# Cross-attention's sums sent whole through DRAM, their reciprocals broadcast back, and the last projection one turn later

## The reference

```python
x = _layernorm(x + attn(x))                  # 16 heads of 16, causal, projections in and out
x = _layernorm(x + xattn(x, ctx_2048))       # see below
x = _layernorm(x + ffn(x))                   # 256 -> 1024 -> 256, ternary weights, 8-bit activations
# xattn: here the 64 POSITIONS are the channels and the 256 columns the tokens
q = rotary(split_heads(Wq @ x + bq)); k = rotary(split_heads(Wk @ c + bk)); v = split_heads(Wv @ c + bv)
p = softmax(q @ k.T / sqrt(8))               # 8 heads of 8 channels, 256 x 256
out = Wo @ merge_heads(p @ v) + bo
```

## Time and profile before

| | us |
|---|---|
| median of 3 runs (lowest, highest) | 562.46 (562.35, 567.57) |
| the profiled execution | 563.8 |
| its span, first to last instruction | 561.9 |
| mean granted TensorE clock in it | 0.848 of full speed |

### The profile page before, as it was taken

How to read it: one execution, slowest core, us unless ns; L and a number is a source line. 1 busy time by engine, 2 the same in 40 slices (tenths; PEclk the granted TensorE clock), 3 DMA queues, 4 the chain that set the end, 5 groups by cost and what they waited for, 6 DMA issues and landing times. The chain is left out here.

```text
span 561.9 us, 12026 instructions
## 1 busy us (share of the span) xinstructions
PE 450.6 (80%) x4162; PEld 243.0 (43%) x4162; DVE 442.4 (79%) x965; ACT 382.0 (68%) x698; POOL 289.6 (52%) x387
## 2 busy tenths in 40 slices
PE   6568799999999999999999999889877701555563
PEld 5354545555545555555555555433333200333342
DVE  2656687888988979889889798865848959999973
ACT  2222266767767667676676686687767787999972
POOL 5742565447555574475555744620032727667652
PEclk9677799999999999999999999975987875555555
DMA  6134318233242242332422323210000000000010
GB/s 217 48 97 149 97 46 248 66 92 91 57 111 67 64 110 60 90 91 60 108 69 64 106 61 82 71 56 1 3 1 1 1 0 1 10 28 19 30 37 29
DMA packets 51674, 37.07 MB, mean 66 GB/s; under 512 B 21408, under 2 KB 47648, under 8 KB 51488
## 3 DMA queue, kind: packets, MB, share of 16 engines
q1 hardware_dynamic: 51328, 36.10, 22.8%
q10 hardware_dynamic: 288, 0.23, 0.2%
HBM read 24.52 MB, written 10.49 MB: 62 GB/s over the span
## 5 line engine op out<-in xcount | busy, mean ns | idle before, releaser
L970 DVE TENSOR_REDUCE MX<-mx_b 128x2 f32<-128x512 f32 x256 | 167.8, 679 | 37.6 <-PE mx_b L581 36.4
L775 ACT ACTIVATE PB<-e_b 128x512 f32<-128x512 f32 x256 | 149.6, 592 | 64.7 <-PE e_b L609 63.8
L581 PE MATMUL mx_b<-KA,QA 48*128 48x256 bf16 x512 | 100.8, 282 | 10.3 <-DVE MX L970 10.1
L609 PE MATMUL e_b<-QA,KA 50*128 50x256 bf16 x512 | 100.9, 281 | 2.7 <-ACT PB L775 2.1
L626 PE MATMUL u_b<-PB,VA 128*32 128x256 f32 x1024 | 86.2, 404 | 3.4 <-ACT PB L775 2.9
L897 POOL TENSOR_TENSOR SP<-SP,srec 128x1024 f32<-128x1024 f32 x15 | 28.5, 1901 | 79.0 <-DVE srec L942 79.0
L581 PEld LDWEIGHTS mx_b<-KA,QA 48*128 48x128 bf16 x512 | 30.1, 95 | 88.5 <-issue 48.9
L1238 POOL TENSOR_TENSOR H<-H,row_tab 128x1024 f32<-128x1024 f32 x16 | 37.8, 2359 | 22.9 <-ACT H L1196 19.5
L1285 PE MATMUL r_b<-identh,Q 128*128 128x128 f16 x128 | 16.6, 311 | 39.5 <-ACT Q L1206 39.5
L1291 PE MATMUL z_b<-w2q,Q2T 128*128 128x256 bf16 x128 | 30.2, 417 | 19.3 <-ACT Q2T L1217 19.3
L314 POOL TENSOR_TENSOR rs<-mv,epsc 128x1 f32<-128x1 f32 x32 | 6.1, 189 | 72.5 <-DVE mv L301 50.2
(11 more groups left out here) (169 smaller groups left out, 1048.4 us busy)
## 6 DMA issues: line engine op xcount, KB each, us to landing
KA<-parts_k SPq DMA_DIRECT2D x64, 96.0 KB
QA<-parts_q SPq DMA_DIRECT2D x64, 96.0 KB
parts_q<-part_q SPq DMA_DIRECT2D x32, 128.0 KB, 2.0
parts_k<-part_k SPq DMA_DIRECT2D x16, 192.0 KB, 2.1
C<-in_ctx SPq DMA_DIRECT2D x16, 128.0 KB, 3.0
X<-in_x SPq DMA_DIRECT2D x16, 128.0 KB, 2.9
out_y<-O SPq DMA_DIRECT2D x16, 128.0 KB, 1.7
XT<-in_xT SPq DMA_DIRECT2D x15, 128.0 KB, 2.2
```

Of the source, the lines that this page charges most:

```text
L581: m = nc.tensor.matmul(mx_b[n % 2][:, D * k:D * k + D], QA[low:low + K_MAX, 2 * i.ring + b, h, P * u:P * u + P], KA[low:low + K_MAX, 2 * i ...
L609: m = nc.tensor.matmul(e_b[n % 2][:, D * k:D * k + D], KA[low:low + K_EXP, 2 * i.ring + b, h, P * sc:P * sc + P], QA[low:low + K_EXP, 2 * ...
L775: nc.scalar.activation(PB[:, n % 4].rearrange("p e t -> p (e t)"), e_b[n % 2][:, :], ACT.Exp, scale=XC ** -0.5).then_inc(e_sb.sem, 1)
L970: nc.vector.tensor_reduce(MX[:, b, e, 2 * q:2 * q + 2, u], mx_b[n % 2][:, :].rearrange("p (e s) -> p e s", e=2), AXL.X, ALU.max).then_inc( ...
```

## The change

1. `u_transpose`, `u_norm`, `att_transpose` and `at_copy` are gone. US goes whole to a DRAM tensor `u_hbm` of (32, 4, 2, 512), one DMA of 256 KB per sequence. When both have landed, one row of each group of 32 is loaded as S32 (the sums, 128x32) and eight as UV (the values, 128x256). VectorE takes reciprocals of S32 at step 6 of the next turn; they go out to DRAM (16 KB) and come back broadcast over 8 channels as RB (128x256). GpSimd multiplies UV by RB (`means`).
2. The columns of the output projection's weights are reordered on the host, and the value bias goes through the projection once, in turn 0, into the bias `xbo` (`value_bias`).
3. The projection and the second norm come one turn later, for `late` = i-2: projection at step 5, statistics at step 6, `norm2` and `square_sum` at step 9, `norm2_max` at step 10. In turn 15 they come a second time, for pair 14: steps 12, 13, 15, 15. On GpSimd `rstd` of late stands ahead of `self_norm`, and `means` of prev behind it.
4. On SyncE the new DMAs and their waits stand between the old ones; the expansion of k opens the next turn, that of q comes ahead of `max_rows(nxt, 0)`.
5. In the feed-forward block the last pair's load, reciprocals (VectorE, turn 2), projection (turn 6), statistics (turn 7) and norm (turn 8) come later; the factors at turn 13 instead of 9.
6. `identb` is built by two copies of 64 rows instead of one addition.

```diff
@@ functions of both phases @@
-        def u_transpose(pe, i, b, ps):
...
-        def att_transpose(pe, i, ps):
...
-        def at_copy(act, i, g):
...
-        def u_norm(dve, i, b, g):
...
+        u_hbm = nc.dram_tensor("u_hbm", (32, 4, 2, 2 * D), F32, kind="Internal").ap()
+        rec_hbm = nc.dram_tensor("rec_hbm", (16, D), F32, kind="Internal").ap()
+        def store_sums(sp, i, b):
+            if has(i, 1):
+                sp.wait_ge(ld_uv, 16 * i.v)
+                sp.wait_ge(ld_us, 16 * i.v)
+            wait(sp, u_sb, i, b + 1)
+            sp.dma_start(u_hbm[:, :, b].rearrange("c j x -> j c x"), US[:].rearrange("p s t -> p (s t)")).then_inc(moved[b], 16)
+
+        def load_sums(sp, i):
+            if has(i, 1):
+                wait(sp, at_sb, i.plus(-1), 1)
+            for b in range(2):
+                sp.wait_ge(moved[b], 16 * (i.v + 1))
+            flat = u_hbm.rearrange("c j b x -> c (j b x)")
+            sp.dma_start(S32[:], flat[XC:XC + 1].rearrange("c (r t) -> (c r) t", t=32)).then_inc(ld_us, 16)
+            sp.dma_start(UV[:], flat[0:XC].rearrange("c (r t) -> (c r) t", t=D)).then_inc(ld_uv, 16)
+
+        def recip_out(sp, i):
+            wait(sp, u_rec, i, 1)
+            if has(i, 1):
+                sp.wait_ge(rec_in, 16 * i.v)
+            sp.dma_start(rec_hbm.rearrange("h (k t) -> (h k) t", t=32), S32[:]).then_inc(rec_out, 16)
+
+        def recip_in(sp, i):
+            sp.wait_ge(rec_out, 16 * (i.v + 1))
+            sp.dma_start(RB[:], rec_hbm.unsqueeze(0).broadcast_to([XC, 16, D])).then_inc(rec_in, 16)
+
+        def reciprocals(dve, i):
+            dve.wait_ge(ld_us, 16 * (i.v + 1))
+            nc.vector.reciprocal(S32[:], S32[:]).then_inc(u_rec.sem, 1)
+
+        def means(pool, i):
+            pool.wait_ge(ld_uv, 16 * (i.v + 1))
+            pool.wait_ge(rec_in, 16 * (i.v + 1))
+            if has(i, 1):
+                wait(pool, xo_ps, i.plus(-1), 1)
+            nc.gpsimd.tensor_tensor(AT[:], UV[:], RB[:], ALU.mult).then_inc(at_sb.sem, 1)
@@ SyncE, body(i) @@
+                if real(prev):
+                    store_sums(sp, prev, 1)
+                if i.v >= 0 and real(j):
+                    expand_rows("k", j)
                 if i.v >= 1 and real(a):
                     load_c(a)
+                if real(prev):
+                    load_sums(sp, prev)
                 if real(i):
                     max_rows(i, 1)
                 if real(a):
                     cross_values(a)
+                if real(prev):
+                    recip_out(sp, prev)
                 if real(j):
                     store_parts("q", j)
+                if real(prev):
+                    recip_in(sp, prev)
+                if real(i):
+                    store_sums(sp, i, 0)
+                if real(j):
+                    expand_rows("q", j)
                 if real(nxt):
                     max_rows(nxt, 0)
-                if real(j):
-                    expand_rows("q", j)
...
-                if real(a):
-                    expand_rows("k", a)
@@ TensorE, body(i) @@
+                    if s == 5 and real(late):
+                        x_out_proj(pe, late, use(g_b[2], ln2, late, 1))
+                    if s == 12 and i.v == NPAIR - 1:
+                        x_out_proj(pe, prev, use(g_b[2], ln2, prev, 1))
@@ ScalarE, u_copy @@
-                    wait(act, ut_ps, i, 1)
+                    act.wait_ge(moved[0], 16 * (i.v + 1))
@@ ScalarE, body(i) @@
+                    if s == 9 and real(late):
+                        norm2(act, late)
+                        square_sum(act, late)
@@ VectorE, body(i) @@
+                    if s == 6 and real(prev):
+                        reciprocals(dve, prev)
+                    if s == 6 and real(late):
+                        norm2_stats(dve, late, 2)
+                    if s == 10 and real(late):
+                        norm2_max(dve, late)
@@ GpSimd, body(i) @@
+                if real(late):
+                    rstd(pool, ln2, late, mv2, rs2)
                 if real(a):
                     self_norm(pool, nc.gpsimd, a)
+                if real(prev):
+                    means(pool, prev)
                 if i.v == NPAIR - 1:
                     mean_power(pool, 0)
-                if real(prev):
                     rstd(pool, ln2, prev, mv2, rs2)
```

More of the change, by code:

```diff
@@ L629, in pv_quad, with value_bias @@
                 last.then_inc(pv.sem, 1)
+            def value_bias(g):
+                ps = use(g_b[g], Event(s_bias, 0), Pair(0, 0), 1)
+                pe.wait_ge(ld_cross, NCROSS)
+                nc.tensor.matmul(ps[:, 0:1], xw["o"], xb["v"], start=True, stop=True).then_inc(s_bias_ps, 1)
             def weight_total(g):
@@ L869, in body @@
                         v_copy(i.plus(4), g_b[0])
-                    if s == 15 and real(prev):
+                    if s == 15 and i.v == NPAIR - 1:
+                        norm2(act, prev)
                         square_sum(act, prev)
@@ L995, in _ @@
             dve.wait_ge(ld_att, 16)
-            nc.vector.tensor_tensor(identb[:].rearrange("p (b t) -> p b t", b=2),
-                                    ident[:, 0:HALF].unsqueeze(1).broadcast_to([P, 2, HALF]),
-                                    ident[:, HALF:P].unsqueeze(1).broadcast_to([P, 2, HALF]), ALU.add).then_inc(s_tab, 1)
+            for r in range(2):
+                own = slice(HALF * r, HALF * r + HALF)
+                nc.vector.tensor_copy(identb[own, :].rearrange("p (b t) -> p b t", b=2),
+                                      ident[own, own].unsqueeze(1).broadcast_to([HALF, 2, HALF])).then_inc(s_tab, 1)
             nc.vector.tensor_copy(maskb[:], mask.unsqueeze(1).broadcast_to([P, 8, SEQ])).then_inc(s_tab, 1)
             def body(i):
-                prev, nxt, j, a = i.plus(-1), i.plus(1), i.plus(2), i.plus(3)
+                late, prev, nxt, j, a = i.plus(-2), i.plus(-1), i.plus(1), i.plus(2), i.plus(3)
                 for s in range(16):
@@ L1221, in _ @@
                 first_values(t)
-                if t == 1:
-                    at_copy(act, last, 0)
-                if t == 5:
+                if t == 8:
                     norm2(act, last)
@@ L1251, in _ @@
             mean_power(pool, 1)
+            means(pool, last)
             rstd(pool, ln2, last, mv2, rs2)
-            mean_power(pool, 2)
             for n in range(NPAIR):
+                if n == 5:
+                    mean_power(pool, 2)
                 wait(pool, qb, Pair(0, n), 1)
@@ L1406, in _ @@
         def _(sp):
+            load_sums(sp, last)
+            recip_out(sp, last)
+            recip_in(sp, last)
             for n in range(NPAIR):
@@ L1450 @@
         own = np.arange(64 * b, 64 * b + 64)
+        summed = np.arange(XC * 4 * 2 * 2).reshape(XC, 4, 2, 2)[:, :, b].reshape(-1)
         for k, n in enumerate(XW):
-            cross_w[64 * b:64 * b + 64, k, split[b] if n in ROTATED else own] = weights[n].T
+            cols = split[b] if n in ROTATED else own
+            cross_w[np.ix_(summed if n == "o" else own, [k], cols)] = weights[n].T[:, None, :]
         for k, n in enumerate(XBIAS):
-            cross_b[split[b] if n in ROTATED else own, k] = biases[n]
+            cross_b[split[b] if n in ROTATED else summed if n == "v" else own, k] = biases[n]
     arrays = {
```

111 lines of the change are left out of this document (40 added, 71 removed).

## The result

The changed kernel takes 622.17 us (median of 4 runs, 618.0 to 625.56) against 564.62 (4 runs, 562.35 to 567.57) for the kernel before on the same chip: a ratio of 1.101, 95% interval 1.090 to 1.112. Slower was right; the size was not. I had forecast 577 us with a range up to 590, so the loss is 57.5 us where 14.6 were reckoned.

The account below looks back on a forecast made before the run. It took TensorE and VectorE as both full in a turn's first half, TensorE alone in the second. Terms -0.5 + 3.5 + 7.0 + 0 - 2.5 + 5.9 + 1.2 = +14.6 us gave 577 us, range 558 to 590.

Parts of the forecast that it names:

- The store: SyncE's 256 KB store of US: confined to 4 engines, 73 GB/s, landing 4.7 us after issue (bounds 2.0 and 7).
- It fits, with half a microsecond: Middle turns: sums and row maxima arrive in time despite the store, the sums with a margin of 0.5 us.
- behind the keys' expansion on the same engines: Load of the sums in a middle turn: there by 10.0 us into the turn, queued after the keys' expansion.
- Late sums: Rival, chance 0.13: data come a microsecond later, VectorE stands at step 6 every turn, +1 x 11, 588 us.
- The per-turn term: Each of eleven middle turns: 1.82 us longer in one half, 1.18 shorter in the other, +0.64 net, +7.0 in all.
- ScalarE hides its part: Rival, chance 0.20: step 12 is not held up by ScalarE, a turn grows 0.1 rather than 0.64 us, 571 us.
- first half: Steps 5 to 12 of a turn, TensorE and VectorE both full: self-attention's transposes start later, +1.82 us.
- The ends: Outside the middle turns: turn 0 -0.5, turn 1 +3.5, turn 13 0, turn 14 -2.5, turn 15 +5.9, feed-forward +1.2 us.
- TensorE was the only bound: Rival, chance 0.17: step 6's statistics fit into waits, a turn gains 1.3 of 1.55 us, 548 us by the median.

Follow-up runs that it names:

- e4: Changed kernel in which SyncE no longer waits for the stores and the loads of sums and values read constant tables instead: 616.02 us, ratio 1.093.
- b1: Kernel before plus only the stores of US to DRAM, in the pattern led by 4, read by nothing: 599.73 us, ratio 1.068.
- b2: As b1, the kernel before plus stores nobody reads, but with the DRAM pattern led by 128: 565.43 us, ratio 1.000.
- e1: Changed kernel with each store of US cut into four DMAs of 32 partitions: 582.63 us, ratio 1.033.
- e3: Changed kernel with the four stores of e1 and the late norm put back to its old steps: 567.82 us, ratio 1.006.
- e8: e3 with stores of 9 of each 32 partitions and the identity built by one addition: 561.83 us, ratio 0.997 against the kernel before.
- e9: e8 with the load of the values issued behind the row maxima instead of ahead: 559.34 us, ratio 0.995 against the kernel before.

## Why the prediction failed, step by step

- *The store.* Right: a quarter of the engines (share 0.25), and that a microsecond more would be felt in every turn. The step that failed is "It fits, with half a microsecond". The landing was taken as 4.7 us after the issue; it was 5.8 idle and 7.3 in a middle turn, where the expansion of the keys and C are issued behind it. Within that term the rate was taken too low (73 GB/s, measured 96) and the time at both ends much too short (1.1 us, for which no row stood, against 3.1). A margin of 0.5 was set against a term whose own bounds reached 2.3 us higher.
- *What lies behind the store.* The sum priced the store by when it lands and when SyncE may go on. That is the smaller part (e4, without SyncE's wait, is 6 us faster by the medians, with overlapping intervals). The larger one, seen in b1 where nothing waits for the data (35 us by the medians), is that DMAs issued behind it finish late; that their parts share four engines with it is the reading that b1 and b2 leave. The forecast mentions this once ("behind the keys' expansion on the same engines") and prices it for the sums alone; the maxima at step 8, those of the next pair at step 0, and C were left at their old durations. The rival *Late sums*, 588, had the direction but priced one stall per turn, not two or three.
- *The clock.* No rival had TensorE's clock in the middle turns. It is at 0.50 for some us in seven of the eleven (mean 0.93 against 1.00), and four of these are 1 to 4 us longer than the rest. That is the smaller part of the 36 us (28 are there without it, by the estimate above). That the stalls bring the falls isn't shown: e4 waits as often and its middle turns are at 0.98. In turns 12 to 15 the clock is 0.64 against 0.86; before, the last 24 us before the feed-forward block ran at 1.00.
- *The per-turn term.* The mechanism is shown by e1: +0.39 where +0.64 was worked out, from a first half of +1.55 for +1.82 and -1.16 for -1.18. The gap of 0.27 lies on ScalarE: exp 10 ends at E+9.42 (reckoned 9.7), and exp 9 had ended at E+7.76 (reckoned 7.9). So *ScalarE hides its part* doesn't hold either; step 12's product waits for exp 10 there. Times eleven it would have been 4.3 in place of 7.0.
- *Sizes.* The reciprocal of 128x32 lasts 0.34 us and holds VectorE for 0.26 (240.00 to 240.26 in e1), where 0.2 was taken. GpSimd's multiply takes 0.73 (median; 0.7 reckoned). The new build of identb costs VectorE 2.2 us in place of 0.3, but it does lie under an idle stretch: the first score matmul stands at 10.6 us with it (e3) and at 10.8 without (e8).
- *The ends.* Turn 1: e1 shows +3.0 for +3.5, turn 0 -1.1 for -0.5. In the changed kernel turn 0 grew by 2.3 instead, for the store is there too: the chain has 5.06 us of QA<-MR in it. The other 2.4 of the +4.7 stand ahead of turn 0, whose start lies between 71.5 us (b1) and 74.5 (changed) in these profiles. Turns 12 to 15: +17.6 for +4.0; e1, with the store cured, still +11.6, and e3 +4.6. I had booked turns 13 and 14 as 0 and a gain; what the norm's place costs there isn't told apart from the clock (0.86 before, 0.68 in e1, 0.80 in e3). The forecast took all of turn 14 at 0.50, but before, its last third already ran at 1.00. Feed-forward +2.9 for +1.2, and -2.0 in e1: not told apart from the clock.
- *TensorE was the only bound.* Wrong for this code (e1 is slower than before with the data in time), but of the 1.3 us per turn that it speaks of 0.8 are there in e9 (turns 2 to 11 last 21.65 on average), when step 6 is left as it was.

Left open: what sets the clock's falls, in turns 12 to 15 above all, and the part of e8's gain over e3 that no wait accounts for.

## What to carry to other kernels

Price a DMA that runs on few engines twice: by when it lands, and by what every DMA issued within that time will lose on the same engines; the second was the larger here, and no wait in the code shows it. Where the slowest dimension of a tile's pattern is small, split it into DMAs led by a large one, or store only the rows that are read, before anything else is tuned; then look whether the queue has the issue time (0.4 to 0.7 us each here). And where two stages share a full engine, put new work in the half of the turn in which that engine idles: the same norm at steps 5 to 10 and at 9 to 15 differs by 7 us over turns 1 to 11 (e1 and e3).

## What the runs showed of the hardware that I had not expected

- A store of 256 KB whose pattern begins with 4 moves 96 GB/s at a share of 0.25 and needs 5.8 us to land on an idle queue; in four DMAs led by 32 each lands after 1.7 (the last is issued 1.3 us after the first), led by 128 after 2.0 to 2.3 by the medians.
- The identity's blocks, in the group view of the changed kernel:

```profile
L1029 DVE CAST identb<-att_tab 64x128 bf16<-64x128 f32 x2 | 2.1, 1064 | 5.1 <-DMA att_tab<-in_attn_tables 5.0
```

The 1064 ns are a mean of two very different ones: the two casts of 64x128 took 0.30 and 1.83 us, and in every kernel that has them the second takes 1.8. One addition over 128x128 did the whole in 0.29 before. Why one is so long isn't known.
- Half a megabyte more through DRAM in every turn cost nothing when the pattern is led by 128 (b2: 1.000, 0.997 to 1.004), though the DMA share was 0.31 already.
